# A token model's front in one core: first norm and projections by halves of the tokens, loads in another order

## The reference

```python
# token embedding
return W[x] + pe[None, :, :]
# _layernorm, then linear attention
m = jnp.mean(x, axis=axis, keepdims=True)
v = jnp.var(x, axis=axis, keepdims=True)
return (x - m) / jnp.sqrt(v + eps)
q = jnp.einsum('bnc,oc->bno', x, Wq)
kv = jnp.einsum('bnc,oc->bno', x, Wkv)
q = jax.nn.elu(q) + 1.0
k = jax.nn.elu(k) + 1.0
k_sum = k.sum(axis=2)
D_inv = 1.0 / jnp.maximum(jnp.einsum('bhnd,bhd->bhn', q, k_sum), 1e-06)
context = jnp.einsum('bhnd,bhne->bhde', k, v)
attn = jnp.einsum('bhnd,bhde->bhne', q, context) * D_inv[..., None]
# position network of the Toeplitz block: depends on weights alone
h = idx @ pos_w.T + pos_b
for i in range(LAYERS):
    h = jax.nn.relu(_srms(h, RPE)) @ rpe_lw[i].T + rpe_lb[i]
return jax.nn.relu(_srms(h, RPE)) @ out_w.T + out_b
```

## Time and profile before

| | us |
|---|---|
| median of 3 runs | 328.85 |
| the profiled execution's own time | 330.29 |
| its span | 328.5 |
| PE busy in the span | 292.5 |
| DVE busy | 233.4 |
| ACT busy | 148.3 |
| POOL busy | 118.0 |

### The profile page before, as it was taken

One profiled execution on the slowest core, in us unless ns is written; L12 is line 12 of the kernel. 1 busy time (PEld: TensorE's weight loads), 2 busy tenths in 40 slices (PEclk: granted clock), 3 DMA queues, 4 the chain that ended last, 5 costly groups with the idle time before them and its releaser, 6 DMA issues.

```text
span 328.5 us, 4420 instructions
## 1 busy us (share of the span) xinstructions
PE 292.5 (89%) x1556; PEld 166.5 (51%) x1567; DVE 233.4 (71%) x428; ACT 148.3 (45%) x249; POOL 118.0 (36%) x168
## 2 busy tenths in 40 slices
PE   1649989999989999889999999989999999999873
PEld 1315754753423444467655555555564555557552
DVE  1578788889989778567864687844768677675476
ACT  2113634752566677755547444544533111021283
POOL 5774000331661235301412550430105589930212
PEclk9999999999999999979999999999999999999996
DMA  7958300285000000700000000000000000000001
GB/s 249 335 108 351 167 0 0 42 156 94 3 2 2 2 3 1 257 0 2 1 0 0 3 0 2 0 0 0 3 0 0 2 0 0 1 2 0 0 3 64
DMA packets 6270, 15.24 MB, mean 46 GB/s; under 512 B 1384, under 2 KB 3816, under 8 KB 5608
## 3 DMA queue, kind: packets, MB, share of 16 engines
q1 hardware_dynamic: 5685, 14.41, 14.5%
q0 software_dynamic: 512, 0.53, 0.7%
q10 hardware_dynamic: 51, 0.01, 0.0%
HBM read 12.01 MB, written 0.52 MB: 38 GB/s over the span
## 4 chain that ended last, share of the span: by engine, by line
PE 52%; DVE 9%; POOL 4%; ACT 4%; issue 3%; another core or an unknown queue 0%; POOLq 0%; DVEq 0%; ACTq 0%
PE ps L336 48%; DVE arena L1893 1%; PE ps L837 1%; DVE h L2020 1%; POOL share L600 1%; ACT L1217 1%; PE ps L1110 1%; PE ps L881 1%; POOL share L601 1%; ACT arena L1396 1%; DVE xs L1820 0%; POOL rw L493 0%; DVE h L2069 0%; DVE xc L2081 0%
## 5 line engine op out<-in xcount | busy, mean ns | idle before, releaser
L1759 DVE TENSOR_REDUCE rw<-ps 128x1 f32<-128x512 f32 (+2 forms) x80 | 45.8, 628 | 6.9 <-PE ps L336 6.4
L1336 ACT ACTIVATE arena<-ps 128x1024 f32<-128x1024 f32 (+3 forms) x48 | 37.6, 812 | 23.8 <-PE ps L336 23.3
L336 PE MATMUL ps<-arena 96*128 96x512 bf16 (+7 forms) x192 | 43.1, 327 | 0.5 <-DVE rw L1759 0.2
L336 PE MATMUL ps<-xs,e_hi 128*128 128x512 f32 x96 | 40.5, 422 | 1.0 <-ACT arena L1396 0.8
L1396 ACT ACTIVATE arena<-ps 128x512 f32<-128x512 f32 x48 | 28.5, 597 | 28.1 <-PE ps L336 23.8
L1893 DVE TENSOR_TENSOR arena<-ps,arena 128x512 f32<-128x512 f32 x48 | 32.4, 686 | 11.3 <-ACT arena L1396 9.8
L336 PE MATMUL ps<-xs,e_lo 128*128 128x512 f32 x96 | 37.9, 395 | 0.0
L336 PE MATMUL ps<-bfc_s 128*128 128x512 bf16 (+2 forms) x100 | 27.5, 345 | 1.8 <-DVE xc L1616 1.6
L336 PEld LDWEIGHTS ps<-arena 96*128 96x128 bf16 (+1 forms) x192 | 15.8, 97 | 26.0 <-DVE rw L1759 11.6
L507 POOL TENSOR_SCALAR_AFFINE_SELECT arena<-arena 128x256 f32<-128x256 f32 (+1 forms) x32 | 15.1, 473 | 31.2 <-ACT arena L1336 30.9
L336 PE MATMUL ps<-arena,ew 64*64 64x512 f32 (+1 forms) x128 | 24.2, 609 | 1.7 <-issue 1.4
(11 more groups left out here) (273 smaller groups left out, 513.5 us busy)
## 6 DMA issues: line engine op xcount, KB each, us to landing
arena<-arena SPq DMA_DIRECT2D x24, 96.0 KB, 2.8
w<-wpack SPq DMA_DIRECT2D x1, 2089.5 KB, 10.6
arena<-tm SPq DMA_DIRECT2D x2, 1024.0 KB, 5.8
tables<-epack SPq DMA_DIRECT2D x1, 1540.0 KB, 11.3
...
```

The lines of the kernel that those rows point to most:

```text
L336: return nc.tensor.matmul(o, l, r, start=start, stop=stop, **kw)
L1336: nc.scalar.activation(pt[:, n % PT_SLOTS, :, lo:512], ps[:, bank:bank + 2, lo:512], ACT.Exp, scale=HD ** -0.5).then_inc(S("exp_done"), 1)
L1759: V.tensor_reduce(top_view(m, part)[:, at:at + len(heads), i], src, AXX, ALU.max, negate=True).then_inc(S("ring_read"), 1)
```

## The change

Six things change together.

1. The pack `w` has its columns in another order, and its first 784 (`WFRONT`: first projections, their bias, the masks) are loaded by a DMA of their own, on the semaphore of the position table; `bfc_s` comes next, then the other 3395 columns.
2. The rotary tables are issued by SP only when slice 0 has been gathered.
3. The first norm is done by halves: half 0 gets its own root and scale (`first_root`, `first_scale`) as soon as slice 0 is in, half 1 after slices 1 and 2. The eps is added in the activation's bias (`eps1`).
4. DVE's order puts `embed(0)` and the scale of half 0 ahead of the last step of the position network, and ACT's order puts half 0's work between the squares of the slices.
5. PE transposes and projects half 0 before it transposes `r_act`; `keep_warm` has 10 products in place of 14 and waits for the third centred slice.
6. For half 0, ACT makes the negative parts with `Relu` of the negated input; half 1 still has DVE's minimum. POOL's bias addition also waits for `geo`.

```diff
 WCOLS = {}
 _at = 0
-for _n, _w in (("q1", P), ("kv1", 2 * P), ("proj1", P), ("q2", P), ("q2r", P), ("k2", 64), ("k2r", 64), ("v2", 64),
+for _n, _w in (("q1", P), ("kv1", 2 * P), ("proj1", P), ("bproj", P), ("mask_c", P), ("mask_k", 16),
...
+               ("q2", P), ("q2r", P), ("k2", 64), ("k2r", 64), ("v2", 64),
                ("wo2", P), ("v3", 2 * D1), ("u3", 2 * D1), ("o3", 3 * P), ("t3", P), ("w4", P),
-               ("bproj", P), ("ub", 2 * D1), ("vb", 2 * D1), ("ob", 1), ("tb", P), ("b4", P), ("ln2", 1),
-               ("ln1", 1), ("cen", P), ("mask_c", P), ("mask_k", 16), ("eidx", P), ("enum", P)):
+               ("ub", 2 * D1), ("vb", 2 * D1), ("ob", 1), ("tb", P), ("b4", P), ("ln2", 1),
+               ("ln1", 1), ("cen", P), ("eidx", P), ("enum", P)):
     WCOLS[_n] = (_at, _at + _w)
     _at += _w
 WTOT = _at
+WFRONT = WCOLS["mask_k"][1]
 RCOLS = {}
 _at = 0
 for _n, _w in (("lag", 2 * P), ("ones", P), ("l0", P), ("l1", P), ("l2", P), ("pw", 1), ("pb", 1), ("b0", 1), ("b1", 1),
@@ -295,6 +297,7 @@
...
             sp.dma_start(idt[:], ident).then_inc(ld_id, 16)
             sp.dma_start(pe_s[:], pe).then_inc(ld_pe, 16)
-            sp.dma_start(w[:], wpack).then_inc(ld_w, 16)
-            sp.dma_start(rope_s[:], rope).then_inc(ld_rope, 16)
-            for c in range(2):
-                sp.dma_start(rope_k[64 * c:64 * c + 64], rope[0:64, :, c * 512:(c + 1) * 512]).then_inc(ld_rope, 16)
+            sp.dma_start(w[:, 0:WFRONT], wpack[:, 0:WFRONT]).then_inc(ld_pe, 16)
             sp.dma_start(bfc_s[:], bfc).then_inc(ld_bf, 16)
+            sp.dma_start(w[:, WFRONT:WTOT], wpack[:, WFRONT:WTOT]).then_inc(ld_w, 16)
             at = 3 * P + B * NPAIR * P
             for b in range(B):
                 sp.dma_start(kst[MROW:KROWS, b * NKV:b * NKV + NKV].rearrange("p g t -> p (g t)").rearrange("p (n t) -> p n t", t=P),
                              spread(bfc[0:65:32, at:at + P], 1, NKV * N // P)).then_inc(ld_ones, 16)
             for a, (lo, hi) in enumerate(SLICES):
                 sp.wait_ge(gathered[a], 16 * B * (hi - lo))
+                if a == 0:
+                    sp.dma_start(rope_s[:], rope).then_inc(ld_rope, 16)
+                    for c in range(2):
+                        sp.dma_start(rope_k[64 * c:64 * c + 64], rope[0:64, :, c * 512:(c + 1) * 512]).then_inc(ld_rope, 16)
             for s in range(2):
                 sp.dma_start(tm_s[:, s], tm[s]).then_inc(ld_m, 16)
...
             pool.wait_ge(S("n1"), 2)
-            pool.wait_ge(ld_w, 16)
+            pool.wait_ge(S("geo_done"), 2 * NW)
+            pool.wait_ge(ld_pe, 32)
             nc.gpsimd.tensor_tensor(h[:].rearrange("p j b c -> p j (b c)"), h[:].rearrange("p j b c -> p j (b c)"),
                                     spread(W("bproj"), 1, NT), ALU.add).then_inc(S("constants"), 1)
...
+            def first_projections(a):
+
+                pe.wait_ge(S("n1"), a + 1)
+                for j in range(4 * a, 4 * a + 4):
+                    ins = nc.tensor.transpose(ps[:, 2 + a, j % 4 * P:(j % 4 + 1) * P], sq[:, j].rearrange("p b c -> p (b c)"), idt[:])
+                ins.then_inc(S("T1"), 1)
+                pe.wait_ge(ld_pe, 32)
+                pe.wait_ge(S(("xT1_lo", "xT1_hi")[a]), 1)
+                for x in range(2):
+                    for j in range(4 * a, 4 * a + 4):
+                        ins = mm(ps[:, 2 * x + a, j % 4 * P:(j % 4 + 1) * P], xT[:, j * P:(j + 1) * P], W("kv1", x * P, (x + 1) * P))
+                    ins.then_inc(S("kv1"), 1)
+                mm(ps[:, 4 + a], W("q1"), xT[:, a * 512:(a + 1) * 512]).then_inc(S("q1"), 1)
+
+            first_projections(0)
             pe.wait_ge(S("r_act"), LAYERS + 1)
             nc.tensor.transpose(ps[:, 7, 0:P], rh[:, 3, 0:P], idt[:])
             nc.tensor.transpose(ps[:, 7, P:2 * P], rh[:, 3, P:2 * P], idt[:]).then_inc(S("r_T"), 1)
             pe.wait_ge(ld_bf, 16)
-            pe.wait_ge(S("first_centred"), 1)
-            keep_warm(14, 6)
-
-            transposes(sq, 2, S("n1"), S("T1"))
-            pe.wait_ge(ld_w, 16)
-            for x in range(2):
-                for j in range(NT):
-                    if x == 0 and j % 4 == 0:
-                        pe.wait_ge(S(("xT1_lo", "xT1_hi")[j // 4]), 1)
-                    ins = mm(ps[:, 2 * x + j // 4, (j % 4) * P:(j % 4 + 1) * P], xT[:, j * P:(j + 1) * P],
-                             W("kv1", x * P, (x + 1) * P))
-                    if j % 4 == 3:
-                        ins.then_inc(S("kv1"), 1)
-            for c in range(2):
-                mm(ps[:, 4 + c], W("q1"), xT[:, c * 512:(c + 1) * 512]).then_inc(S("q1"), 1)
+            pe.wait_ge(S("first_centred"), 3)
+            keep_warm(10, 6)
+            first_projections(1)
...
+            pe.wait_ge(ld_w, 16)
             mm(ps[:, 6, P:2 * P], W("cen"), W("w4")).then_inc(S("gf"), 1)
...
-            for i in range(LAYERS + 1):
+            def lag_root(i):
+
                 act.wait_ge(S("r_ss"), i + 1)
                 if i >= 1:
                     act.wait_ge(S("r_scale"), i)
...
-            for a in range(len(SLICES)):
-                first_squares(a)
-
-            act.wait_ge(S("mean_squares"), NORMS["var1"])
-            nc.scalar.activation(st[:, 3], st[:, 2], ACT.Sqrt).then_inc(S("roots"), 1)
-            evac(2, S("T1"), 1, S("xT1_lo"))
+
+            def first_root(a):
+
+                act.wait_ge(S("mean_squares"), NORMS["var1"] + a)
+                nc.scalar.activation(st[:, 3, 8 * a:8 * a + 8], st[:, 1, 8 * a:8 * a + 8], ACT.Sqrt, scale=1.0 / C,
+                                     bias=eps1[:]).then_inc(S("roots"), 1)
+
+            def first_columns(a):
+
+                act.wait_ge(S("T1"), a + 1)
+                nc.scalar.copy(xT[:, 512 * a:512 * a + 512], ps[:, 2 + a]).then_inc(S(("xT1_lo", "xT1_hi")[a]), 1)
+
+            def first_values(a):
+
+                act.wait_ge(S("kv1"), 2 * a + 2)
+                nc.scalar.copy(va1[:, 4 * a:4 * a + 4, 0:P], ps[:, 2 + a].rearrange("p (j x) -> p j x", j=4)).then_inc(S("va1"), 1)
+
+            for i in range(LAYERS):
+                lag_root(i)
+            first_squares(0)
+            lag_root(LAYERS)
+            act.wait_ge(S("geo_constants"), 1)
+            first_root(0)
+            first_columns(0)
+            first_squares(1)
+            act.wait_ge(S("kv1"), 1)
+            nc.scalar.activation(kf1[:, 0:4].rearrange("p j b c -> p (j b c)"), ps[:, 0], ACT.Relu, scale=-1.0).then_inc(S("kmin"), 1)
+            first_values(0)
+            act.wait_ge(S("q1"), 1)
+            nc.scalar.activation(qf1[:, 0:512], ps[:, 4], ACT.Relu, scale=-1.0).then_inc(S("qmin"), 1)
+            first_squares(2)
+            first_root(1)
             next_function(ACT.Exp)
-            for a in range(2):
-                act.wait_ge(S("kmin"), a + 1)
-                nc.scalar.activation(kf1[:, 4 * a:4 * a + 4], kf1[:, 4 * a:4 * a + 4], ACT.Exp).then_inc(S("kexp"), 1)
-            for a in range(2):
-                act.wait_ge(S("kv1"), a + 3)
-                nc.scalar.copy(va1[:, 4 * a:4 * a + 4, 0:P], ps[:, 2 + a].rearrange("p (j x) -> p j x", j=4)).then_inc(S("va1"), 1)
-            for c in range(2):
-                act.wait_ge(S("qmin"), c + 1)
-                nc.scalar.activation(qf1[:, c * 512:(c + 1) * 512], tmp[:, c * 512:(c + 1) * 512], ACT.Exp).then_inc(S("qexp"), 1)
+            first_columns(1)
+            act.wait_ge(S("kmin"), 1)
+            nc.scalar.activation(kf1[:, 0:4], kf1[:, 0:4], ACT.Exp, scale=-1.0).then_inc(S("kexp"), 1)
+            act.wait_ge(S("qmin"), 1)
+            nc.scalar.activation(qf1[:, 0:512], qf1[:, 0:512], ACT.Exp, scale=-1.0).then_inc(S("qexp"), 1)
+            act.wait_ge(S("kmin"), 2)
+            nc.scalar.activation(kf1[:, 4:8], kf1[:, 4:8], ACT.Exp).then_inc(S("kexp"), 1)
+            first_values(1)
+            act.wait_ge(S("qmin"), 2)
+            nc.scalar.activation(qf1[:, 512:N], tmp[:, 512:N], ACT.Exp).then_inc(S("qexp"), 1)
...
+            act.wait_ge(ld_w, 16)
             evac(2, S("T2"), 1, S("xT2_lo"), scale=W("ln1"))
...
+            V.memset(eps1[:], 1e-5)
             V.memset(geo[:], 0.0).then_inc(S("geo_constants"), 1)
...
-            for i in range(LAYERS + 1):
+            def first_scale(a):
+
...
+                step(V.reciprocal(hst(4, a), hst(3, a)))
+                V.tensor_tensor(half3(sq, a), half3(xc, a), spread(hst(4, a), 2, C), ALU.mult).then_inc(S("n1"), 1)
...
+            def first_total(a):
+
+                lo, hi = SLICES[a]
+                dve.wait_ge(S("first_squared"), a + 1)
+                V.tensor_reduce(st[:, 1, B * lo:B * hi], sq[:, lo:hi].rearrange("p j b c -> p (j b) c"), AXX,
+                                ALU.add).then_inc(S("mean_squares"), 1)
+
+            for i in range(LAYERS):
                 rpe_layer(i)
-            dve.wait_ge(ld_pe, 16)
+            dve.wait_ge(ld_pe, 32)
             embed(0)
```

(45 more changed lines are left out.)

13 lines of the change are left out of this document (7 added, 6 removed).

## The result

| | before | after |
|---|---|---|
| median of 20 runs | 329.01 (328.54 to 330.61) | 330.85 (329.00 to 331.46) |
| ratio after / before | | 1.0037, 95% interval 1.0022 to 1.0052 |
| profiled execution, its span | 330.29, 328.5 | 329.34, 327.6 |

The change made the kernel 1.2 us slower by the ratio (0.0037 x 329; 0.7 to 1.7 by its interval), against +0.7 forecast. The median itself, 330.85, lies above the forecast's own range (328.8 to 330.4) and inside the wide one (327.4 to 331.0).

A forecast was written before the change was run, and what follows sets the result against it. DVE was taken to hold the front up to T, then PE up to `cbd`; +2.6 at T and -1.6 behind it gave +1.0, or +0.1 with faster queries; +0.7 taken, 329.6 us, own range 328.8 to 330.4, wide 327.4 to 331.0.

The forecast's parts named there:

- T: End of the scale of half 1, normed halves complete: 29.37 us before, forecast 32.0, or 31.1 if PE's rate doubles before the queries.
- ACT's order: Slice 2's squares stand behind the Relu of half 0's queries on ACT; 3.0 us from queries' end to T.
- the squares directly behind the `Relu`: Sign of being right: ACT's squares of slice 2 come just behind a Relu, with DVE idle before its last sum.
- What bounds the front: DVE busy 7.58 of 8.42 us from 20.98 to 29.40; with the change, half 0 normed at 21.6.
- PE's rate: Half 0's projections run at the lower clock up to the queries: 5.4 us, to 29.0; 2.7 us at full rate.
- What the prediction quotes on transposes: Skill text: transposes do not count as matmul activity for PE's clock; by it the slow end, T = 32.0.
- Loads: Gathers in the front: slice 0 lands nearest 15.5; slice 1, wanted at 21.6, costs nothing if 2.3 us later.
- rival 2: A gathered slice comes late in the front: +1.7, 330.6 us; decides for slice 1 from about 24; chance 0.17.
- Behind T: From T to `cbd`, half the projections already done: 9.12 becomes 7.5 us, a gain of 1.6.
- The sum: Front total: +1.0 with all of half 0 at the lower rate, +0.1 with queries at the upper; +0.7 taken.
- Rival 1: Half 0 runs at speed on PE, T = 29.5 by DVE: `cbd` at 37.0, -1.4 us, 327.4 us; chance 0.24.
- Rival 3: Shift at `cbd` is taken up later by slack of DVE or POOL: 328.85 us; chance 0.08.

The follow-up runs named there:

- experiment 2: Changed kernel with 8 filler products on PE behind the first out projection, rotary tables issued behind slice 2 instead of slice 0: 329.20 us, ratio 0.9994.
- after with fillers: Changed kernel plus 8 filler products on PE behind the first out projection of the causal attention (about 138.7 us): 329.64 us, ratio 1.0009.
- Experiment 3: After with fillers, with ACT's squares of slice 2 ahead of the Relu of half 0's queries: 329.48 us, ratio 0.9999.
- experiments 1: The same 8 mid-kernel PE fillers added to the kernel before (328.74 us, ratio 0.9985) and to the changed kernel (329.64 us, ratio 1.0009).
- experiment 4: After with fillers plus both edits, rotary tables behind slice 2 and slice 2's squares ahead of half 0's Relu: 328.73 us, ratio 0.9975.
- experiment 6: Ten early PE fillers added to after with fillers: 330.89 us; also with both edits of experiment 4: 326.96 us, and 332.54 us when run again.

## Why the prediction was right

The direction, the sign at T, the gain behind it and about the size were right. The size is in part luck: what held T was the late slice 1, and ACT's order behind PE at the lower rate, on which the forecast was built, ended at nearly the same time. With the slice in time it alone gives T = 30.86 (experiment 2), 0.24 below the 31.10 of after with fillers. Of the forecast's own signs, T at 31 to 32 and `cbd` at 38.5 to 39.5 were missed narrowly in the profile of after (30.93 and 38.31) and met to 0.02 us in that with fillers (31.10 and 38.48); the squares directly behind the `Relu` were seen in the second and not in the first. By its steps:

- *What bounds the front.* Half 0 was ready for DVE at 15.80 (16.1 foreseen, slice 0 in at 15.3 against 15.5), normed at 21.12 (21.6), and PE's first projection came at 23.06 (23.65). They are 0.2 to 0.6 early.
- *PE's rate.* The step on which the forecast hung holds: 3.47 us for the 16 instructions, 0.21 apart (0.228 foreseen), and the upper rate from the start of the queries or somewhere in them: 1.02 us for the two in the profile of after, 1.43, 1.40, 1.30 and 1.25 in four of the variants. The point at which the rate doubles differs between executions, as the range between +0.1 and +1.0 said. What the prediction quotes on transposes was not settled by any run here.
- *ACT's order.* Foreseen as what ties T to PE: half right. Experiment 3 takes it away and T is no sooner, since slice 1 was as late. The prediction's 3.0 us from the queries to T was 3.55 in the profile of after (27.38 to 30.93), with the wait of 0.67 for DVE in it; in experiment 2, where ACT's order sets T, it was 2.76 (28.10 to 30.86).
- *Loads.* This is the term that was mis-sized. It said that slice 1 may land 2.3 us behind 21.6 at no cost. It landed at 23.0, 1.9 behind the moment DVE was free (21.1). From `embed(1)` to T it takes the 7.9 us foreseen: 23.03 + 7.9 = 30.93, which is T; 23.22 and 23.49 give 31.10 and 31.38 in experiments 1 and 3, to 0.02. So the mechanism of rival 2 held T in these executions. Its point of decision was set 1 us too late because PE and ACT were expected to be later than they were. Slice 0, rival 2's other half, came in time.
- *What holds T* is thus three things within 0.7 us of each other: slice 1 (30.93), ACT's order and PE (30.86 in experiment 2), and PE's `r_T` behind the queries (30.44 in experiment 4). That is why the edits gave 0.24, nothing, and 0.66 together. These are single profiles; the times agree for both edits together (0.90 by the means) and can't tell for either alone. Only with PE at the upper rate as well was T below that of before: 28.75 against 29.37.
- *Behind T.* 7.5 foreseen, 7.38 measured, in after and in the after with fillers.
- *The sum.* +0.7 foreseen. +0.90 between the two kernels with fillers, +0.5 and +1.1 in the two groups. Their profiles show 0.51 of it at `cbd`, the forecast's, and 0.20 in the wait behind it, which the prediction had at nothing; the rest is not placed.
- *Rival 1* (half 0 at speed, 327.4 us) did not happen in after. It was made to happen in experiment 6. Its condition alone gave 330.89 us, since slice 1 was late; with both edits as well it gave 326.96 us, about what the rival said, but in one comparison of two. *Rival 3* is out: between the two kernels with fillers the shift of 0.51 at `cbd` is 0.71 at 45 us and 0.57 at the end.
- *Not foreseen:* the stretch at 0.50 near 142 us. That it lies in the upper group's runs is shown by their granted clocks and by the fillers that remove both. Why after has it in 12 of 20 runs and before in 8 was not tried; with numbers so small, the two shares may be the same.
